# Another order of work where an MLP and a combination open, and products of zeros on PE

## The reference, cut to what matters

```
x = x + L0_xattn(layernorm(x), ctx)   # attention, convolution over time, MLP (below)
x = x + L0_ffn(layernorm(x))          # router: two of 8 experts per token, 512 rows each at most
x = x + L1_xattn(layernorm(x), ctx)   # attention with 16 heads
x = x + L1_ffn(layernorm(x))          # two of 8 experts per token again

# the end of L0_xattn: the change's first place
y  = s4d(x_mod)                        # a causal convolution of 64 steps in each channel
xt = x_text + y * (1 + gate * scale_out) + gate * shift_out
h  = gelu(layernorm(xt) @ W1 + b1) @ W2 + b2
return layernorm(xt + h) * g + b

# the end of L0_ffn: its second place: the two experts' rows of a token, weighed and summed
y = (eo[ids, pos] * probs * keep).reshape(N, 2, C).sum(axis=1)
```

## Time and profile before

| | us |
|---|---|
| median of 3 runs (930.09 to 934.98) | 931.65 |
| profiled execution, its own time | 925.46 |
| span of the profiled execution, first to last instruction | 924.2 |
| PE, DVE, ACT, POOL busy in the span | 708.5, 677.3, 473.4, 566.2 |
| mean granted clock of PE in the span, as a share of full speed | 0.854 |

### The profile page before, as it was taken

One profiled execution on the slowest core, in us unless ns is written; L12 is line 12 of the kernel. 1 busy time (PEld: TensorE's weight loads), 2 busy tenths in 40 slices (PEclk: granted clock), 3 DMA queues, 4 the chain that ended last, 5 costly groups with the idle time before them and its releaser, 6 DMA issues. The chain is left out here.

```text
span 924.2 us, 20983 instructions
## 1 busy us (share of the span) xinstructions
PE 708.5 (77%) x6340; PEld 521.4 (56%) x6340; DVE 677.3 (73%) x3212; ACT 473.4 (51%) x1318; POOL 566.2 (61%) x932
## 2 busy tenths in 40 slices
PE   0687798889984999953699338988898965799960
PEld 0354565556773666522476236756666652799960
DVE  6898999989543787678021085688999886699974
ACT  3566666756302545430232284587777761577740
POOL 7688877767647444200777576346778767277770
PEclk9887999979995999976699755898989886899995
DMA  6300112896317878400564410000000003698918
GB/s 144 58 25 9 36 52 63 85 91 83 57 47 277 259 252 254 162 11 1 69 125 112 149 62 1 2 2 17 24 24 26 26 30 105 205 277 264 265 59 273
DMA packets 98829, 94.42 MB, mean 102 GB/s; under 512 B 37511, under 2 KB 82302, under 8 KB 98142
## 3 DMA queue, kind: packets, MB, share of 16 engines
q1 hardware_dynamic: 91268, 79.34, 33.2%
q0 software_dynamic: 6592, 13.58, 5.9%
q10 hardware_dynamic: 858, 0.17, 0.1%
HBM read 47.76 MB, written 43.19 MB: 98 GB/s over the span
## 5 line engine op out<-in xcount | busy, mean ns | idle before, releaser
L2415 POOL DMA_INDIRECT expert_pairs<-e_ys,e_home x78 | 75.5, 967 | 38.5 <-issue 23.5
L1755 POOL TENSOR_SCALAR a_kb<-a_kr,a_m,a_bk 128x128 f32<-128x128 f32 x128 | 58.5, 457 | 44.3 <-ACT a_kr L1994 32.2
L1773 POOL DMA_INDIRECT expert_slots<-r_rows,r_slotu x64 | 63.4, 991 | 29.1 <-issue 13.3
L961 DVE MATCH_REPLACE8 work<-m,work 128x64 f32<-128x64 f32 x384 | 75.8, 207 | 0.0
L1497 POOL DMA_INDIRECT ex_rows<-rows,slot_source x32 | 30.8, 963 | 53.3 <-POOLq L1176 43.8
L948 DVE MAX8 m<-work 128x8 f32<-128x64 f32 x384 | 57.1, 209 | 0.0
L1828 PE MATMUL a_pss<-a_kb,a_qt 32*64 32x256 f32 x512 | 41.0, 455 | 14.3 <-ACT a_pp L1979 12.1
L2181 DVE TENSOR_REDUCE a_mx<-a_pss 128x8 f32<-128x512 f32 x64 | 43.9, 685 | 8.1 <-PE a_pss L1828 7.8
L2382 PE MATMUL e_ps<-e_XH,e_wh 128*128 128x256 f32 x156 | 48.2, 309 | 1.5 <-DVE e_XL L2427 1.5
L1549 ACT ACTIVATE ex_hs<-ex_psh,vec 128x512 f32<-128x512 f32 x32 | 22.0, 688 | 51.1 <-PE ex_psh L1530 50.5
L2384 PE MATMUL e_ps<-e_XH,e_wl 128*128 128x256 f32 x156 | 44.7, 287 | 0.0
(11 more groups left out here) (475 smaller groups left out, 2473.3 us busy)
## 6 DMA issues: line engine op xcount, KB each, us to landing
expert_slots<-rt_unfilled SPq DMA_DIRECT2D x151, 130.0 KB, 2.9
ahead<-folded_weights SPq DMA_DIRECT2D x20, 386.0 KB, 3.9
e_wf<-folded_weights SPq DMA_DIRECT2D x19, 386.0 KB, 3.7
planes<-rt_zeros SPq DMA_DIRECT2D x4, 1024.0 KB
ew<-in_L_ffn_ew SPq DMA_DIRECT2D x16, 256.0 KB, 4.0
pair_y<-expert_pairs SPq DMA_DIRECT2D x16, 256.0 KB, 5.8
e_xr<-expert_slots SPq DMA_DIRECT2D x27, 130.0 KB, 3.1
folded_weights<-fold_done SPq DMA_DIRECT2D x8, 384.0 KB, 3.5
```

Of the source, the lines that this page charges most:

```text
L961: return own.did(dve.match_replace(wk_[x.j][:, h, :], m8[x.j][:, h, r, :], src[:, h, :], TAKEN))
L1755: m = pool.tensor_scalar(kb[a.j][:, :, h, :], k, m4[:, h:h + 1], bk4[:, h:h + 1], ALU.mult, ALU.add)
L1773: pool.indirect_dma_start(G.slots, bass.IndirectOffsetOnAxis(ap=slot[:, b, k, t:t + 1], axis=0), rb[b % NB][:, k, t, :], None).then_inc(se ...
L2415: pool.indirect_dma_start(G.pair, bass.IndirectOffsetOnAxis(ap=home[i % NY][:, k:k + 1], axis=0), ys[i % NY][:, k, :], None).then_inc(kept ...
```

## The change

Three places are edited.

1. Behind the last group of the convolution PE makes 20 products of zeros instead of 2.
2. In the MLP, POOL begins with the root of block 0, then the zeros, the root of block 1, the tile `unfilled`, the biases of block 0, the root of block 2, the biases of block 1, then `pick` and the counters, the biases of block 2, and goes on from t = 1 as before. PE opens with 8 products of zeros, 8 more behind the wait for block 0's variance, 6 behind the wait for its root, block 0's transposes, and 4 more; then it makes the hidden products of block 0 ahead of the transposes of block 1. From t = 1 its order is as before. ACT's order follows: GELU of block 0 stands ahead of the copy of block 1.
3. In the combination, DVE makes the constant row `cst` first of all, and ACT makes the three small copies behind the first block's weighing instead of ahead of it.

```diff
--- before.py
+++ after.py
@@ -1047,7 +1047,7 @@
                             mm = pe.matmul(psy[g % 4][rows, c, :], G.toe[rows, g * CH + c, :], G.XM[rows, :, g * CH + c],
                                            start=True, stop=True)
                     mm.then_inc(s["y"], 1)
-                    fill(pe, G, unread, 2)
+                    fill(pe, G, unread, 2 if g + 1 < NG else 20)
 
             @block.vector
             def _(dve):
@@ -1203,6 +1203,26 @@
             @block.gpsimd
             def _(pool):
                 step = Steps(pool, s["pool"])
+
+                def root_of(q, b):
+                    pool.wait_ge(var[q], b + 1)
+                    inverse_root(pool, step, st[q], root[q])
+
+                def add_biases(b):
+                    rows = slice(b * TB, (b + 1) * TB)
+                    pool.wait_ge(s["xs"], b + 1)
+                    pool.tensor_tensor(G.XT[:, rows, :], G.XT[:, rows, :], wide(b2[:].unsqueeze(1), [P, TB, D]), ALU.add)
+                    pool.tensor_tensor(G.X[:, rows, :], G.X[:, rows, :], wide(bout[:].unsqueeze(1), [P, TB, D]), ALU.add).then_inc(s["biased"], 1)
+
+                root_of(0, 0)
+                pool.memset(zeros[:], 0.0).then_inc(s["zeros"], 1)
+                root_of(0, 1)
+                step.did(pool.iota(unfilled_i[:], pattern=[[1, STILE // P]], base=SPARE, channel_multiplier=STILE // P))
+                step.then(pool.memset(unfilled[:], 0.0))
+                pool.tensor_copy(unfilled[:, :, D:D + 1].bitcast(U32).rearrange("p k a -> p (k a)"), unfilled_i[:]).then_inc(s["unfilled"], 1)
+                add_biases(0)
+                root_of(0, 2)
+                add_biases(1)
                 step.then(pool.tensor_tensor(pick[:], G.ident[:, 0:32], G.ident[:, 32:64], ALU.add))
                 for c in range(2, NH):
                     step.then(pool.tensor_tensor(pick[:], pick[:], G.ident[:, 32 * c:32 * c + 32], ALU.add))
@@ -1210,37 +1230,44 @@
                 pool.iota(count_i[:], pattern=[[1, P]], base=0, channel_multiplier=0).then_inc(s["counts"], 1)
                 pool.iota(name_i[:], pattern=[[B * T, 2], [1, NT]], base=1, channel_multiplier=NT).then_inc(s["counts"], 1)
                 pool.iota(spare_i[:], pattern=[[P, NS2]], base=1 + 2 * B * T, channel_multiplier=1).then_inc(s["counts"], 1)
-                pool.memset(zeros[:], 0.0).then_inc(s["zeros"], 1)
-                step.did(pool.iota(unfilled_i[:], pattern=[[1, STILE // P]], base=SPARE, channel_multiplier=STILE // P))
-                step.then(pool.memset(unfilled[:], 0.0))
-                pool.tensor_copy(unfilled[:, :, D:D + 1].bitcast(U32).rearrange("p k a -> p (k a)"), unfilled_i[:]).then_inc(s["unfilled"], 1)
-                for t in range(-2, NBLK + 1):
+                add_biases(2)
+                for t in range(1, NBLK + 1):
                     for q, b in ((0, t + 2), (1, t - 1), (2, t - 1)):
                         if blk(b):
-                            pool.wait_ge(var[q], b + 1)
-                            inverse_root(pool, step, st[q], root[q])
+                            root_of(q, b)
                     if blk(t + 2):
-                        rows = slice((t + 2) * TB, (t + 3) * TB)
-                        pool.wait_ge(s["xs"], t + 3)
-                        pool.tensor_tensor(G.XT[:, rows, :], G.XT[:, rows, :], wide(b2[:].unsqueeze(1), [P, TB, D]), ALU.add)
-                        pool.tensor_tensor(G.X[:, rows, :], G.X[:, rows, :], wide(bout[:].unsqueeze(1), [P, TB, D]), ALU.add).then_inc(s["biased"], 1)
+                        add_biases(t + 2)
 
             @block.tensor
             def _(pe):
-                for t in range(-1, NBLK + 3):
+                def turn_first(b):
+                    pe.wait_ge(s["xs"], b + 1)
+                    after(pe, s["xf"], b)
+                    after(pe, s["xf1"], b - 3)
+                    for k in range(TB):
+                        mm = pe.transpose(pst[:, k * P:(k + 1) * P], xs[b % 2][:, k, :], G.ident[:])
+                    mm.then_inc(s["turned"], 1)
+
+                def hidden(b):
+                    pe.wait_ge(s["xf"], b + 1)
+                    for c in range(NH):
+                        after(pe, r_sb[c], b - 2)
+                        pe.matmul(psh[c][:], w1[:, c * P:(c + 1) * P], xf[b % 2][:], start=True, stop=True).then_inc(h_ps[c], 1)
+
+                fill(pe, G, psg[:, 0:2 * P], 8)
+                pe.wait_ge(var[0], 1)
+                fill(pe, G, psg[:, 0:2 * P], 8)
+                pe.wait_ge(root[0], 1)
+                fill(pe, G, psg[:, 0:2 * P], 6)
+                turn_first(0)
+                fill(pe, G, psg[:, 0:2 * P], 4)
+                for t in range(NBLK + 3):
+                    if t == 0:
+                        hidden(0)
                     if blk(t + 1):
-                        j = (t + 1) % 2
-                        pe.wait_ge(s["xs"], t + 2)
-                        after(pe, s["xf"], t + 1)
-                        after(pe, s["xf1"], t - 2)
-                        for k in range(TB):
-                            mm = pe.transpose(pst[:, k * P:(k + 1) * P], xs[j][:, k, :], G.ident[:])
-                        mm.then_inc(s["turned"], 1)
-                    if blk(t):
-                        pe.wait_ge(s["xf"], t + 1)
-                        for c in range(NH):
-                            after(pe, r_sb[c], t - 2)
-                            pe.matmul(psh[c][:], w1[:, c * P:(c + 1) * P], xf[t % 2][:], start=True, stop=True).then_inc(h_ps[c], 1)
+                        turn_first(t + 1)
+                    if 0 < t < NBLK:
+                        hidden(t)
                     if blk(t - 3):
                         b = t - 3
                         after(pe, s["lg"], b)
@@ -1300,15 +1327,24 @@
             @block.scalar
             def _(act):
                 act.preload_act_table(ACT.Gelu)
-                for t in range(-1, NBLK + 3):
+                def keep_first(b):
+                    act.wait_ge(s["turned"], b + 1)
+                    act.activation(xf[b % 2][:], pst[:], ACT.Identity, scale=G.vec[:, gv:gv + 1],
+                                   bias=G.vec[:, bv:bv + 1]).then_inc(s["xf"], 1)
+
+                def gelu(b):
+                    for c in range(NH):
+                        act.wait_ge(h_ps[c], b + 1)
+                        act.activation(hs[b % 2][:, c, :], psh[c][:], ACT.Gelu, bias=G.vec[:, b1 + c:b1 + c + 1]).then_inc(h_sb[c], 1)
+
+                keep_first(0)
+                for t in range(NBLK + 3):
+                    if t == 0:
+                        gelu(0)
                     if blk(t + 1):
-                        act.wait_ge(s["turned"], t + 2)
-                        act.activation(xf[(t + 1) % 2][:], pst[:], ACT.Identity, scale=G.vec[:, gv:gv + 1],
-                                       bias=G.vec[:, bv:bv + 1]).then_inc(s["xf"], 1)
-                    if blk(t):
-                        for c in range(NH):
-                            act.wait_ge(h_ps[c], t + 1)
-                            act.activation(hs[t % 2][:, c, :], psh[c][:], ACT.Gelu, bias=G.vec[:, b1 + c:b1 + c + 1]).then_inc(h_sb[c], 1)
+                        keep_first(t + 1)
+                    if 0 < t < NBLK:
+                        gelu(t)
                     if blk(t - 3):
                         b = t - 3
                         act.wait_ge(s["logits"], b + 1)
@@ -1948,11 +1984,13 @@
                 act.activation(wot[:], psc[:, 256:384], ACT.Copy)
                 act.wait_ge(cm["opened"], 2)
                 act.activation(cstt[:], psd[:, 0:P], ACT.Copy).then_inc(cm["cst_turned"], 1)
-                act.wait_ge(cm["opened"], 3)
-                act.activation(cols[:], psc[:, 0:NE], ACT.Copy)
-                act.activation(wo[:, D:DE], psc[:, 32:32 + NE], ACT.Copy)
-                act.activation(cst[:, D:DE], psc[:, 64:64 + NE], ACT.Copy).then_inc(cm["extra"], 1)
                 ident = ACT.Identity
+
+                def keep_constants():
+                    act.wait_ge(cm["opened"], 3)
+                    act.activation(cols[:], psc[:, 0:NE], ACT.Copy)
+                    act.activation(wo[:, D:DE], psc[:, 32:32 + NE], ACT.Copy)
+                    act.activation(cst[:, D:DE], psc[:, 64:64 + NE], ACT.Copy).then_inc(cm["extra"], 1)
 
                 def weigh_rows(b):
                     act.wait_ge(fetched[b], 2 * 16)
@@ -2032,6 +2070,8 @@
 
                 for b in range(NBLK):
                     weigh_rows(b)
+                    if b == 0:
+                        keep_constants()
                     if b >= 3:
                         keep_rows_turned(b - 3)
                 act.wait_ge(s["ready"], 1)
@@ -2064,6 +2104,8 @@
                 shape = [P, TB, NE]
                 iota = wide(G.iota8[:].unsqueeze(1), shape)
 
+                dve.wait_ge(cm["rows_of"], 1)
+                dve.tensor_tensor(cst[:, 0:D], G.att["bo"][:], psd[:, 0:D], ALU.add).then_inc(cm["cst"], 1)
```

(2 more changed lines are left out.)

## The result

| | before | changed |
|---|---|---|
| median (lowest to highest), us | 930.87 (927.07 to 934.98), 4 runs | 915.11 (909.81 to 921.51), 4 runs |
| profiled execution: span, own time | 924.2, 925.46 | 908.6, 909.81 |

What follows compares the result with a forecast made beforehand. No engine bounds the whole span; at each place the chain ending last counts, in the MLP's opening mostly DVE's and POOL's. 5.2 + 3.2 - 1.1 = 7.3 off the median 931.65 gives 924.4, range 918.5 to 930.5.

Steps and rivals of the forecast that it cites:

- The MLP's opening: From block 0's statistics to its normalised output: POOL's new order brings the chain over DVE and POOL 3.2 us earlier.
- memset's hold: MLP's opening: POOL's memset of zeros holds up DVE's first normalising until it ends; without this, 4.7 us saved, not 3.2.
- the normalising beside the biases: MLP's opening: DVE's normalising beside POOL's two bias additions takes 3.03 us where it takes 1.09 alone.
- the row: Profile row in the MLP: DVE's normalisation beside POOL's root took 1.09 us, as alone; the forecast went by it.
- the port rule: Whichever of a GpSimd and a fast DVE instruction starts first holds their shared ports throughout; saving in the MLP's opening 2.4.
- The clock in PE's new gap: MLP: PE idles about 3.2 us before block 0's output; a clock fall costs up to 2.2, middle 1.1 taken.
- Products of zeros: PE behind the convolution and at the MLP's opening: the added products neither gain nor cost by themselves, 0.
- The combination: DVE's constant first and ACT's three copies behind the first weighing bring the stage 5.2 us earlier (4.8 to 5.2).
- Rival 3: Second attention: the half-clock stretch may change length; 7 us more gives 927.6, 16 undo the change; chance 0.22.
- the last of the sum: Whole kernel: 7.3 off the profiled 925.46 gives 918.2; put on the runs' median 931.65, it gives 924.4.
- the second attention's clock: Second attention: its first 21 us at half clock should move with the stage's start, so no term in the sum.

Runs made afterwards that it cites:

- combination only: The kernel before with only the combination's part of the diff, convolution and MLP as before: 920.41 us, ratio 0.9909.
- few products behind: The changed kernel with 2 products of zeros behind the convolution's last group in place of 20: 918.99 us, ratio 0.9908.
- late zeros: The changed kernel with POOL's clearing of the zeros behind a wait for block 0's normalised rows: 917.1 us, ratio 0.9897.
- the kernel with the additions beside the statistics: Changed kernel, POOL's bias additions split beside DVE's statistics, zeros late, block 3's root earlier, 2 products behind the convolution, 6 ahead: 916.18 us, again 913.04.

## Why the prediction came out wrong

**The MLP's opening** was right: 3.2 predicted, 3.4 measured in the mean, link by link (root 1.48, memset's hold, 3.0 for the normalising beside the biases). Block 3's normalising beside POOL's root (293.03) took 1.12, so here too the row, and not the port rule of the Trainium skill's "SBUF — State Buffer", section "SBUF: two separate sides", held for that small operand.

**The clock in PE's new gap** costs 1.0 to 1.1 where it falls. That this equals the 1.1 is luck, for the 1.1 was the middle between nothing and 2.2. And it comes or stays away: PE goes from block 0's output to the start of the last logits in 90.4, as before the change, in three of nine profiles with this opening and in 91.4 to 91.5 in six. In the changed kernel's second profile the products behind the same gap run slower than after:

```profile
321.84 1.12 PE L1284 MATMUL mlp_pst<-ident,XT 128*128 128x128 f32 x4 [2.88 <-DVE XT L217]
322.75 4.85 PE L1291 MATMUL mlp_psy<-mlp_w,mlp_hs 128*128 128x128 f32 x32
```

**Products of zeros** at 0: right, behind the convolution and at the opening. The price beside it, 0.167 each from twelve in 2.00, was a little high: six put the convolution off by 0.87, 0.145 each.

**The combination**: 5.2 predicted. The weighing came 5.3 earlier and the first sum 5.3, but the second pair landed 5.9 after its issue (511.68 to 517.55), 1.0 late and not 0.4. Over eleven profiles with the edit (all but the one with more products in the first attention), the stage takes 38.1 to 39.2 against 43.0 to 43.1: 4.4 (mean 38.65).

**Rival 3 failed in its sign.** The sum let the half-clock stretch move with the stage, and the rival gave 0.14 of its 0.22 to one over 6 us longer. It came shorter in nine of eleven profiles. Windows from 51 to 64 us behind the combination's start, of before, after and combination only:

```profile
573.00:586.00 13.00, 13.00 (x124) 10.05 (x124) 4.94 (x13) 6.75 (x22) 3.38 (x8) 0.50 0.01 1
```

```profile
561.40:574.40 13.00, 13.00 (x174) 10.56 (x178) 7.25 (x14) 6.29 (x21) 3.58 (x8) 0.66 0.01 3
```

```profile
579.00:592.00 13.00, 12.64 (x234) 9.72 (x238) 9.98 (x23) 8.85 (x27) 3.71 (x9) 1.00 0.01 3
```

Half clock in the first, partly and wholly full in the others. In five profiles with the old combination the clock rises 64.0 to 64.3 behind the start, in eleven with the new one 50.1 to 60.0. Part of that is the stage's own 4.4: counted from the second attention's first maximum, the stretch lasts 20.9 to 21.3 in the five, 20.9 to 21.1 in two of the eleven, of which the changed kernel's first profile is one (first window below), 18.1 to 18.5 in five and 11.9 to 12.4 in four.

```profile
549.30:570.20 20.90, 19.45 (x166) 14.19 (x167) 9.79 (x21) 10.79 (x34) 7.48 (x15) 0.50 0.01 2
570.20:583.20 13.00, 12.93 (x248) 9.74 (x246) 10.34 (x25) 7.79 (x25) 4.92 (x9) 1.00 0.01 4
```

What decides between the three lengths no run shows. The second attention takes 184.9 in the mean in place of 186.9, though 187.0 in that first profile, and the two stages together 223.6 in place of 229.9: 6.3, not 5.2.

**The step that failed** is the last of the sum: the saving was set against one profiled execution and put on the median of three runs, with their spread of 4.9 as all that chance could do. Beside it, one term was put at nothing that measured 1.9: the second attention's clock.

By the corrected terms the change is worth 3.4 + 6.3 - 0.7 (1.1 in six of nine) = 9.0, which from 931.65 would have been 922.7, inside the range; the median of all 28 executions, 921.4, is inside it too. The ratios of the six measurements with both openings (three of the changed kernel, and those with few products behind, with late zeros and without the MLP's products) average 0.9903, 9.0 of 930; they lie between 0.9851 and 0.9964, so that the agreement to a tenth is chance. Nor does the 0.7 stand in full: from the opening's end to the combination the nine profiles take 209.3 in the mean, five with the old opening 209.1, and why 0.5 of it comes back is open. The mechanism was right and its size 1.7 short.

The other 6.8 of the 15.8 is in no stage that the change edits: the first measurement's profile has the shortest first attention seen. In 16 profiles in which that stage is the same code it takes 204.15 to 215.69, longer the lower its mean granted clock (correlation -0.83). Windows over the stage, of after and of the kernel with the additions beside the statistics (the first of its two runs):

```profile
33.10:237.20 204.10, 172.79 (x889) 115.33 (x888) 191.62 (x1629) 127.20 (x475) 161.18 (x346) 0.90 0.39 58
```

```profile
33.20:248.80 215.60, 185.36 (x874) 123.67 (x871) 192.85 (x1629) 125.86 (x470) 160.92 (x346) 0.82 0.43 55
```

That all four of those runs were such lucky ones is inferred: the other three have no profile. The two shortest of the 16, 204.15 and 206.41, both belong to the changed kernel, so that its program favours them is not excluded; its second profile, 210.88, shows only that it does not bring them every time.

## What to carry to other kernels

Compare two profiles stage by stage before believing a total: the edited stages here repeated to 0.2 and 1.1 while an unedited one moved by 11 us and another by 13. When a few products of zeros can keep a stage of small products from opening at half clock, put them ahead of the stage, where they cost 0.9 and seem to save 13 now and then, not behind it. Beside DVE's normalising, POOL's large additions and clearings held it up until they ended (3.0 and 2.38 in place of 1.1), beside its statistics they did not (0.87): the order on the helper engine alone was worth 6.7 us at one opening (30.25 to 23.5) without one instruction of its own fewer.

## What the hardware showed unexpectedly

The convolution's products (64x32) with two products of zeros behind each group keep full clock all through the stage (granted 1.00, 2.06 a group) and also leave half clock as it is from the second group on (0.50, 3.63 a group), with PE busy 21.41 of 22 us in the one case (the changed kernel with six products ahead) and 26.00 of 26 in the other:

```profile
258.00:280.00 22.00, 21.41 (x546) 19.89 (x542) 10.31 (x16) 0.00 (x0) 9.27 (x8) 1.00 0.19 49
```

And the first attention spreads over 11.5 us between executions of one and the same code.
